# A two-layer AdaLN transformer on one core: ScalarE takes loads, biases and splits in the projections, values lose their padding, loads of the experts go first, and small score blocks share a bank

## The reference

```python
# both layers: x += ga * attn(h); x += gb * ffn(h), h = layernorm(x)*(1+c)+s, s, c, g from a modulation
# layer 0, attention: 16 heads of 8, relative positions
xn = layernorm(x) * ln_g + ln_b
q, k, v = xn @ Wq + bq, xn @ Wk + bk, xn @ Wv + bv
pos = relative_shift((q + v_bias) @ (pe @ Wp).T)
out = softmax(((q + u_bias) @ k.T + pos) * 8**-0.5) @ v @ Wo + bo
# layer 0, ffn: two shared experts (their mean) and 8 experts, two of them weighted per token
shared = mean_s(gelu(xf @ sW1 + sb1) @ sW2 + sb2)
y = shared + sum_e w[t, e] * (gelu(xf @ W1[e] + b1[e]) @ W2[e] + b2[e])
# layer 1, attention: causal and differential, 8 heads of two halves of 8
attn = softmax(q @ k.T * scale + causal)        # 16 score matrices of 512 x 512 a sequence
o = (attn[0::2] - lam * attn[1::2]) @ v, normalized per head, then @ Wo.T
# layer 1, ffn: one expert with relu, then a layer norm
```

## Time and profile before

| | |
|---|---|
| median of three runs | 2532.14 us (2531.35 to 2536.93) |
| the profiled execution | 2532.68 us, span 2530.9 us |
| mean granted TensorE clock | 0.933 |
| busy over the span | TensorE 2171.6 us (86%), VectorE 1642.4 (65%), ScalarE 1332.3 (53%), GpSimd 707.1 (28%) |

### The profile page before, as it was taken

One profiled execution on the slowest core, in us unless ns is written; L12 is line 12 of the kernel. 1 busy time (PEld: TensorE's weight loads), 2 busy tenths in 40 slices (PEclk: granted clock), 3 DMA queues, 4 the chain that ended last, 5 costly groups with the idle time before them and its releaser, 6 DMA issues. The chain is left out here.

```text
span 2530.9 us, 50478 instructions
## 1 busy us (share of the span) xinstructions
PE 2171.6 (86%) x16122; PEld 1283.9 (51%) x16250; DVE 1642.4 (65%) x3386; ACT 1332.3 (53%) x2282; POOL 707.1 (28%) x573
## 2 busy tenths in 40 slices
PE   3663999999999999999849998999997498899586
PEld 1331677777777777777624444444443244444232
DVE  3885788888888888888634343443433688888354
ACT  1220566666666666666525445545453155555454
POOL 1443544444444444444102221222123000000000
PEclk9775999999999999999969999999998699999799
DMA  4443111111111111111020212202211222222221
GB/s 172 138 149 120 36 41 39 39 39 39 39 39 39 42 39 40 40 41 37 17 83 21 71 63 92 87 33 80 74 67 51 67 81 81 87 83 71 88 79 42
DMA packets 94927, 163.61 MB, mean 65 GB/s; under 512 B 18120, under 2 KB 44242, under 8 KB 93586
## 3 DMA queue, kind: packets, MB, share of 16 engines
q1 hardware_dynamic: 94866, 162.82, 20.4%
HBM read 102.37 MB, written 60.41 MB: 64 GB/s over the span
## 5 line engine op out<-in xcount | busy, mean ns | idle before, releaser
L1131 ACT ACTIVATE prob<-prob,neg_max_h 128x640 f32<-128x640 f32 x512 | 425.5, 831 | 325.4 <-DVE neg_max_h L1031 324.8
L1031 DVE CUSTOM_DVE_ANT_0 prob<-pair,pair_mask 128x640 f32<-128x640 f32 x512 | 419.1, 819 | 137.5 <-PE pair L948 136.3
L1607 PE MATMUL pair<-hid,down_w 128*128 128x512 f32 x640 | 309.6, 630 | 30.2 <-DVE moe L1392 25.0
L1910 ACT ACTIVATE prob_h<-pair 128x256 f32<-128x256 f32 (+3 forms) x512 | 205.7, 436 | 193.5 <-PE pair L1797 186.8
L1094 POOL TENSOR_TENSOR a_full<-rot_c,rot_s 128x512 f32<-128x512 f32 x128 | 163.2, 1275 | 500.5 <-DVE rot_s L1018 500.5
L1038 DVE TENSOR_TENSOR prob<-prob 128x128 f32<-128x128 f32 x512 | 272.5, 532 | 0.5 <-ACT prob L1131 0.5
L1533 ACT ACTIVATE hid<-pair,up_b 128x512 f32<-128x512 f32 x320 | 200.8, 691 | 128.7 <-PE pair L1587 128.4
L1849 DVE TENSOR_REDUCE row_max<-pair 128x1 f32<-128x128 f32 (+3 forms) x512 | 221.3, 485 | 54.8 <-PE pair L1776 50.3
L904 PE MATMUL outsum<-ident,prob 128*128 128x128 f32 x1024 | 249.7, 275 | 3.9 <-ACT prob_t L1139 0.5
L904 PE MATMUL turn<-ident,prob 128*128 128x128 f32 x1024 | 250.4, 275 | 0.1
L1607 PEld LDWEIGHTS pair<-hid,down_w 128*128 128x128 f32 x640 | 125.8, 201 | 188.6 <-issue 159.8
(11 more groups left out here) (268 smaller groups left out, 4453.8 us busy)
## 6 DMA issues: line engine op xcount, KB each, us to landing
vx_d<-vx SPq DMA_DIRECT2D x16, 1024.0 KB, 4.8
o_d<-out_sb SPq DMA_DIRECT2D x64, 256.0 KB, 2.0
w_all<-w_d SPq DMA_DIRECT2D x8, 2048.0 KB, 7.2
val<-vx_d SPq DMA_DIRECT2D x32, 256.0 KB, 6.6
val_h<-vx_d SPq DMA_DIRECT2D x32, 256.0 KB
qs_d<-part_q SPq DMA_DIRECT2D x48, 128.0 KB
ks_d<-part_k SPq DMA_DIRECT2D x48, 128.0 KB
num<-o_d SPq DMA_DIRECT2D x24, 256.0 KB
```

The lines of the kernel that those rows point to most:

```text
L1031: nc.vector.tensor_tensor_reduce(prob[s % 4][:, :], pair[:, cols], pair_mask[:, cols], -1.0, 3.0e38, ALU.add, ALU.min, neg_max[par][:, s:s ...
L1131: nc.scalar.activation(prob[s % 4][:, :], prob[s % 4][:, :], ACT.Exp, bias=neg_max[par][:, s:s + 1], scale=-1.0).then_inc(exp_done.sem, 1)
L1607: mm = nc.tensor.matmul(out_ap, down_w[:, EXPERTS[i], c, :], hid[i % 2][:, c, :], start=(c == 0 and i != 1), stop=(c == HC - 1 and i != 0))
L1910: nc.scalar.activation(prob_h1[jb % 2][:, h, jb * P:S], bank[u % EXP_BANKS][:, jb * P:S], ACT.Exp, scale=SCALE).then_inc(h1_exp_used.sem, 1)
```

## The change

*Projections.* The loads of x and of the modulation are issued from ScalarE's queue in place of SP's. ScalarE copies x out of PSUM, adds the three biases (as an activation with scale and a bias that is scaled in the setup) and writes the first part of q straight from PSUM. VectorE keeps the edge product, the normalizations, the two later parts of q and the three of k; these come after the affines. On VectorE a part is made by a cast and no longer by a product with ones.

*Values.* `vx` and `vx_d` hold 8 columns a head, without ones and zeros. The two memsets of `vx` go; `load_val` writes 8 of 32 columns of `val`, and four memsets on GpSimd set the others once.

*Experts.* SP issues the loads of the batch ahead before `spread_weights`, with the load of the modulation apart (`load_mod0`) after it. VectorE makes `moe` before the merge.

*Layer 1's heads.* The blocks of several heads share a bank where they fit in 512 columns: 11 items in place of 16 for the maxima, 11 in place of 16 for the exponentials. The mask is added first, by one product for all heads of an item. The maxima come negated out of the reduction; ScalarE copies the turned maxima and the sums in VectorE's place. TensorE's interleave follows the new items. The core of the diff:

```diff
-        vx_d = dram("vx_d", [NG, P, NB * GH * 32])
+        vx_d = dram("vx_d", [NG, P, NB * GH * DH])
...
-            vec_e.tensor_tensor(qu_bias[:, :], col["bq"], col["u"], ALU.add).then_inc(setup_dve, 1)
+            vec_e.tensor_scalar(qu_bias[:, :], col["bq"], col["u"], SCALE, ALU.add, ALU.mult).then_inc(setup_dve, 1)
...
+            if eng is nc.vector:
+                eng.tensor_copy(parts[i][:, :], src[:, :]).then_inc(steps.sem, 1)
...
         def proj_v(v):
             def body(adaln_of, norm_of, project_of):
-                if adaln_of is not None:
-                    x_t(adaln_of)
...
                 if project_of is not None:
-                    biases(project_of)
-                    for i in range(3):
-                        qu_part(i, project_of)
+                    edge_products(project_of)
...
                 if project_of is not None:
-                    for i in range(3):
-                        k_part(i, project_of)
+                    rest_parts(qu, part_q, rest_q, "qu", project_of)
+                    v.wait_ge(k_stored.sem, k_stored.at(stack_dmas * project_of))
+                    split(v, ve, kt, part_k, rest_k, p2_dve, "k", project_of)
...
         def proj_a(act):
+            def x_t(b):
+                act.wait_ge(p0_pe.sem, p0_pe.at("x_t", b))
+                act.wait_ge(xt_stored.sem, xt_stored.at(16 * b))
+                act.wait_ge(p0_dve.sem, p0_dve.at("a_center", b - 1))
+                nc.scalar.copy(xt[:, :], bank[4][:, :]).then_inc(p0_act.sem, 1)
...
+            def biases(b):
+                act.wait_ge(p2_pe.sem, p2_pe.at("q", b))
+                act.wait_ge(p2_dve.sem, p2_dve.at("qu_r1", b - 1))
+                nc.scalar.activation(qu[:, :], bank[0][:, :], ACT.Identity, bias=qu_bias[:, :], scale=SCALE).then_inc(p2_act.sem, 1)
...
+                act.wait_ge(p2_dve.sem, p2_dve.at("k_r1", b - 1))
...
+            def first_parts(b):
+                act.wait_ge(qu_stored.sem, qu_stored.at(stack_dmas * b))
...
             def body(adaln_of, norm_of, project_of):
+                if adaln_of is not None:
+                    x_t(adaln_of)
+                    if not isinstance(adaln_of, int) or adaln_of + 1 < B:
+                        load_x(adaln_of + 1)
                 if norm_of is not None:
                     ln1.square(act, "b", norm_of, p1_dve, p1_act)
                 if adaln_of is not None:
                     ln0.square(act, "a", adaln_of, p0_dve, p0_act)
+                    load_mod(adaln_of)
+                if project_of is not None:
+                    biases(project_of)
...
+                    first_parts(project_of)
                     values(project_of)
                     edges(project_of)
...
             def load_val(sp, g, par):
-                sp.dma_start(val[par][:, :, :, :].rearrange("p t h d -> p (t h d)"), one(vx_d, g)).then_inc(val_loaded[par].sem, 16)
+                sp.dma_start(val[par][:, :, :, 0:DH], one(vx_d, g).rearrange("p (t h d) -> p t h d", t=NB, h=GH)
+                             ).then_inc(val_loaded[par].sem, 16)
...
+                    nc.gpsimd.memset(val[i][:, :, :, DH:2 * DH], 1.0).then_inc(heads_init, 1)
+                    nc.gpsimd.memset(val[i][:, :, :, 2 * DH:32], 0.0).then_inc(heads_init, 1)
...
             def both(b, ahead, behind):
+                if ahead is not None:
+                    loads(ahead)
                 spread_weights(b)
                 if ahead is not None:
-                    loads(ahead)
+                    load_mod0(ahead)
...
             def both(b, ahead, behind):
+                shared(b)
                 if ahead is not None:
                     merge(ahead)
-                shared(b)
...
-        UNITS = NB * GH
+        MAX_ITEMS = [(0, 0, 4), (1, 0, 2), (1, 2, 2)] + [(ib, h, 1) for ib in (2, 3) for h in range(GH)]
+        EXP_ITEMS = [(jb, h, 1) for jb in (0, 1) for h in range(GH)] + [(2, 0, 2), (2, 2, 2), (3, 0, 4)]
...
             def max_item(n, k, r, m):
+                nc.tensor.matmul(dst[:, :, i0:w], identb[:, :], mask_low.unsqueeze(1).broadcast_to([P, heads, P]),
+                                 start=True, stop=False, skip_group_check=True)
+                for x in range(heads):
+                    mm = nc.tensor.matmul(dst[:, x, :], q_h1[k][0:KM, h0 + x, i0:w], k_h1[k][0:KM, h0 + x, 0:w],
+                                          start=False, stop=(x == heads - 1), skip_group_check=True)
...
-                        for _ in range(min(2 - s % 2, UNITS - m)):
-                            max_unit(*ahead, m)
+                        for _ in range(min(2 if s < 4 else 1, NM - m)):
+                            max_item(*ahead, m)
...
+                    ve.tensor_reduce(row_max1[:, h0:h0 + heads, ib], src, AX_X, ALU.max, negate=True
+                                     ).then_inc(h1_max_used.sem, 1)
...
+            def sums(g):
+                act.wait_ge(h1_pv_done.sem, h1_pv_done.at(NB * (g + 1)))
+                act.wait_ge(h1_stored.sem, h1_stored.at(16 * g))
+                nc.scalar.copy(out_sb1[:, :], out_bank[:, :]).then_inc(h1_copied.sem, 1)
...
+                for u in range(NU):
+                    exp_item(g, k, u)
+                    if u == 2 and not first:
+                        sums(g - 1)
+                    if u == NU - 2 and not last:
+                        negated(g + 1)
```

More of the change, by code:

```diff
@@ L668, in values @@
                 for t in range(NB):
-                    last = nc.scalar.copy(vx[:, :, t, :, 0:DH],
+                    last = nc.scalar.copy(vx[:, :, t, :, :],
                                           bank[3][:, t * P:(t + 1) * P].rearrange("p (g h d) -> p g h d", g=HG, h=GH))
@@ L692, in body @@
                 if project_of is not None:
+                    first_parts(project_of)
                     values(project_of)
                     edges(project_of)
-            act.wait_ge(p_init, 4)
+            act.wait_ge(p_init, 2)
+            load_x(0)
             for t in range(PROJ_STAGES - 1):
                 body(*elements(t, PROJ_STAGES))
-            with act.Fori(PROJ_STAGES - 1, B) as t:
+            with act.Fori(PROJ_STAGES - 1, B - 1) as t:
                 body(*elements(t, PROJ_STAGES))
-            for t in range(B, B + PROJ_STAGES - 1):
+            for t in range(B - 1, B + PROJ_STAGES - 1):
                 body(*elements(t, PROJ_STAGES))
@@ L1733, in build @@
         h1_stored = Count("h1_stored")
-        UNITS = NB * GH
+        MAX_ITEMS = [(0, 0, 4), (1, 0, 2), (1, 2, 2)] + [(ib, h, 1) for ib in (2, 3) for h in range(GH)]
+        EXP_ITEMS = [(jb, h, 1) for jb in (0, 1) for h in range(GH)] + [(2, 0, 2), (2, 2, 2), (3, 0, 4)]
+        NM, NU = len(MAX_ITEMS), len(EXP_ITEMS)
+        UP_TO = [1 + max(u for u, item in enumerate(EXP_ITEMS) if item[0] == jb) for jb in range(NB)]
         def following(g, k, r):
@@ L1870, in group @@
-            def group(g, k, r, first=False):
+            def group(g, k, r):
                 ahead = following(g, k, r)
                 if ahead is not None:
-                    row_maxima(ahead[0], 0)
-                if not first:
-                    sums(g - 1)
-                if ahead is not None:
-                    for h in range(1, GH):
-                        row_maxima(ahead[0], h)
+                    row_maxima(ahead[0], ahead[1])
                     negatives(ahead[0], ahead[1])
@@ L1889, in h1_v @@
                                    identb[KM:KM + GH, KM + h:KM + h + 1].broadcast_to([GH, S])).then_inc(h1_init, 1)
-            for h in range(GH):
-                row_maxima(0, h)
+            row_maxima(0, 0)
             negatives(0, 0)
             for k in range(H1_BUFS):
-                group(k, k, 0, first=(k == 0))
+                group(k, k, 0)
             with v.Fori(1, NG // H1_BUFS - 1) as r:
```

195 lines of the change are left out of this document (95 added, 100 removed).

## The result

The changed kernel takes 2465.69 us (median of four runs, 2463.85 to 2470.37) where the kernel before takes 2532.51 beside it: a ratio of 0.9736, with a 95% interval of 0.9718 to 0.9754. The forecast was 2451 in a range of 2415 to 2486. The profiled execution took 2466.63 us; its span is 2464.5, 66.4 less than before, at a mean granted clock of 0.943. The forecast spoke of 81.

A forecast was written before the change was run, and what follows sets the result against it. VectorE's queue was taken to bound the projections, TensorE's waits for moe and slow clock the experts, TensorE and VectorE layer 1; -27 - 37 - 17 = -81 from 2532.68 gave 2451 us, range 2415 to 2486.

The forecast's parts named there:

- the projections, -27: Projections and start of first layer's heads: before the loop -2, six passes -20, end -6, heads +0.8.
- the first rival: Experts: the wait moves to ScalarE, whose exponentials wait for the merge; -14 there, 2475 us; chance 0.17.
- Against that, VectorE loses cover: Projections pass: only the edge product stands between centring and normalization, leaving 4.3 us of new idle time behind ScalarE.
- the two old waits: Projections pass: VectorE's waits for the mean of x and for q go, 2.6 us.
- The casts: Projections pass: five parts become plain casts on VectorE, two beside GpSimd and three alone, saving 1.5 us.
- The slack that the forecast gave the stored x: Projections: ScalarE wants the stored x's buffer only after its edges, most of a pass after SP issues the store.
- I take -6: Projections after the last centring: stores queue behind fewer bytes of values; -6 us, bounds 0 to -12.
- 26 us of a load: First layer's heads: counting each piece as 512 bytes, a load takes some 26 us, still hidden; the sum stays.
- With moe ahead of the merge: Experts: VectorE makes moe once the shared experts are done, TensorE's 25.0 us of waits go; -37 for the stage.
- -17 forecast: Layer 1: VectorE's shorter list removes about half of TensorE's waits, 0.55 us a group; bounds 0 to -33.
- TensorE's floor: Layer 1 rival: a group falls to TensorE's busy time of 9.91 us; -33 there, 2436 us; chance 0.12.
- Biases on ScalarE: Projections rival: biases stretch ScalarE's chain by 4.7 us a pass, 28 in all; 2480 us; chance 0.04.

The follow-up runs named there:

- q early: Changed kernel with VectorE making the two later parts of q between normalizations and affines: 2453.04 us, projections end at 214.3.
- k early: Changed kernel with VectorE making the parts of k right behind the edge product, their store first and q's last: 2442.90 us, projections end at 208.4.
- the values first: Changed kernel with TensorE making the values' projection right behind those of q and k, ahead of the two variances: 2459.42 us.
- padded values: Changed kernel with values stored with ones and zeros again, vx's two memsets back, loads of 128 rows of 2 KB, GpSimd's four memsets gone: 2467.67 us.
- sums and negated copy: Changed kernel with VectorE again copying layer 1's sums and turned, negated maxima, shared items kept: 2472.25 us, 10.70 us a group.

## Why the forecast was right, and where it was not

*The sum.* The direction and the range held; the size, 81, came out as 66, because one term failed: the projections, -27 with bounds of -5 to -48, gave -7.8 - 1.7 + 3.8 + 2.4 = -3.3, outside their own bounds. The experts and layer 1 gave 9.2 us more than forecast and made up for a part of it, so it is partly luck that 66 is as near to 81 as it is. By the forecast's own sign, a pass that stays over 20 us, it was wrong in the projections: 20.1 in the mean. The upper end of the range, 2486, does not follow from the forecast's terms: the first rival with the projections at their least gain (5 in place of 27) would be 2475 + 22 = 2497.

*The pass.* The step that failed is "Against that, VectorE loses cover". It asked what the parts of q had hidden and found the reciprocal root. They had hidden a second wait behind it, the affine's for the values' projection. VectorE's work (13.6) and the new idle time behind ScalarE (4.3; measured 4.4) came out right in size, the latter with some luck: the chain holds 0.60 us in which ScalarE itself waits for TensorE's slow variance (105.17 above), which the forecast did not have, and ScalarE's operations, which overlap, take some 0.8 less than their sum. The affine's wait, 8.6 us over the six passes or 1.4 each, was left out. That is most of the 2.1 us by which a pass gained less than forecast (1.3 for 3.4); the rest is that in the mean over the six VectorE's work fell by 4.9 in place of 5.1 and the two old waits had been 2.3 in place of 2.6, and 0.1 more of ScalarE's. The list of waits of the kernel before could not show the affine's wait, because its cover was complete; the code has it (the affine waits for the values' projection, `v_x`). The runs with q early and with k early show it: with cover over it, the passes take 18.9 and 17.5 us. The casts gave 0.8 us of VectorE's work a pass and not 1.5; that its sum still came out nearly right means that the rest gave 4.1 where 3.6 stood. GpSimd's seven operations took 8.45 us in place of 9.58, which suggests that less of the two lay side by side than counted. The slack that the forecast gave the stored x was not there: ScalarE's copy of x waits 2.24 us for that store in the pass shown, but VectorE waits for nothing behind it.

*The end of the stage.* "I take -6" had the wrong sign. The forecast looked at the bytes of the values and not at what moved. The parts of q went behind the affines, so the next-to-last store of q is issued 15.3 us after the last centring (196.46) where it was 9.7 (200.24 before), the store of qv behind it on SP 17.1 us after it and not 12.6, and GpSimd's last split, which waits for that store, starts at 26.3 in place of 22.5: these are the 3.8 us. After:

```profile
189.81 1.14 DVE L451 TENSOR_SCALAR xn<-ln_normed,vec 128x512 f32<-128x512 f32 x1 [3.06 <-PE pair L739]
...
196.46 1.73 SPq L360 DMA_DIRECT2D qs_d<-part_q  x3
...
198.23 2.27 SPq L360 DMA_DIRECT2D qv_d<-part_qv  x3
...
207.42 1.04 POOL L464 TENSOR_TENSOR part_qv<-qv,ones_col 128x512 bf16<-128x512 f32 x1 [8.77 <-DMA qv_d<-part_qv]
```

Before:

```profile
200.24 2.90 SPq L360 DMA_DIRECT2D qs_d<-part_q  x3
...
203.19 3.29 SPq L360 DMA_DIRECT2D qv_d<-part_qv  x3
...
213.07 1.04 POOL L461 TENSOR_TENSOR part_qv<-qv,ones_col 128x512 bf16<-128x512 f32 x1 [7.36 <-DMA qv_d<-part_qv]
```

The affine, which now stands ahead of the parts of q, waits for the values' projection here too, 3.06 us. Either edit undoes the 3.8: with the values first, and the parts of q where they are, the end takes 44.0 us, as before; with the parts of q early 40.2, 3.9 less than before.

*The first layer's heads.* No transfer of values is waited for, as forecast; the Trainium skill's page "DMA: Bandwidth & Descriptors", Specifications, by which transfers under 512 bytes fall below line rate, would have made 26 us of a load by the forecast's estimate, and the trace has 6.1. They took 2.4 us more, not 0.8. SP's first load is issued 6.2 us after the first memset (235.23) where it was 5.4, which are the 0.8 of the four memsets; the rest, 0.5 to 1.6 over the runs, is not explained. Neither the memsets nor the small pieces make it: the run with padded values has neither and still takes 1.4 us more than the one trace of the kernel before.

*The experts.* The size was near (-42.8 for -37), and TensorE's waits for moe went, but the step "With moe ahead of the merge" gave the gain to the wrong edit. The forecast's own estimate had the loads landing at 1398 to 1401, before moe can start at 1401.9. By that the merge (2 us) would have fitted in ahead of moe in any order, or nearly, and the conclusion was not drawn. The rival that moves the wait to ScalarE is real (20.4 us) where the loads come late.

*Layer 1.* -17 forecast, -20.4 measured, 10.4 us a group forecast and measured. That the size fits is partly luck, for the mechanism came apart differently: the shared maxima, 0.75 us of VectorE's sum, are worth nothing, and the shared exponentials, to which the forecast gave no gain, are worth up to 0.36 with what goes with them, and without them ScalarE's two copies cost more than they bring (12.3 us a group). TensorE's floor (9.91) was not reached.

*Biases on ScalarE.* 0.68 to 0.69 us each, as taken; that rival is out. The Trainium skill's page "ScalarE: Activation LUTs", Rules for kernel authors, gives additions and multiplications to VectorE; for this shape, f32 out of PSUM, the traces have ScalarE at 0.68 and VectorE at 0.75.

## What to carry to other kernels

Work that is moved off an in-order engine takes its cover along: list every wait behind the place that it leaves, not the first one only, and look in the code for those that the profile can't show because they were covered. What is left then wants a new order: filling the hole with work that is ready (here the parts of k) gave 20.6 us, where the move itself had taken 5.6 off the stage. Of two edits that aim at one wait, try each alone: here the order of the loads did all, and the order of the operations, worth 22 us by itself, added nothing to it.

## What the runs showed of the hardware

Out of PSUM, ScalarE is the quicker copier: 128x512 f32 in 0.58 us (line 1927 after) where VectorE took 0.68, and 4x512, cast to bf16, in 0.58 for 0.70 (VectorE in the run with sums and negated copy there). A cast of 128x512 f32 to bf16 on VectorE takes 0.41 to 0.43 us alone and 1.15 to 1.26 beside GpSimd, a product 0.69 and 1.41 to 1.64. Both lose 0.7 to 1.0 us to GpSimd, so a cast loses more in proportion. The Trainium skill's page "SBUF — State Buffer", section "SBUF: two separate sides", says that the two engines share a pair of ports that one of them holds for a whole instruction; the two lengths agree with that (GpSimd's own operations in the pass shown take 1.04 to 1.39 us).
